# A first expert stage whose output products run as three f32r passes over split operands

## The chip, the cores and the metric

The kernel runs on one core of a Trainium2 chip. The metric is the device time of one execution in microseconds, the median of several runs. A core has TensorE (PE, with its weight loads shown as PEld), VectorE (DVE), ScalarE (ACT) and GpSimd (POOL); SyncE (SP) issues transfers. Each engine works through its own list in order, and they meet at semaphores.

## What is computed

Four pairs of attention and feed-forward layers over x of 8 x 256 tokens with 256 features. What matters here is the first feed-forward layer, a router with eight experts, one of which each token takes:

```python
logits = jnp.einsum('bsd,de->bse', x, router_W) + router_b
top1 = jnp.argmax(softmax(logits), axis=-1)
h = jax.nn.relu(jnp.einsum('bsd,edf->besf', x, W1) + b1[:, None, :])   # 256 -> 1024
y = jnp.einsum('besf,efd->besd', h, W2) + b2[:, None, :]               # 1024 -> 256
out = jnp.einsum('bse,besd->bsd', gates, y)
```

All of it is float32. The second attention, which follows, uses weights wq, wk, wv, wo that are split into a high part (rounded to the one-pass format f32r) and a low part (what rounding lost).

## The kernel before

The kernel is a row of stages, each a block in which all engines start and end together. The first expert stage is `expert_tiles` with `gated=False` and the tag `f0_`; the second expert stage is the same function with `gated=True`, and the change leaves that one alone.

`dispatch` sorts the tokens by expert into NT = 23 tiles of 128 places, each of one expert (`table` holds the expert of each tile, `order` the tokens), and loads the weights of the first two tiles (`load_first`). The weights have two slots; tile i uses slot i % 2. For each tile:

- GpSimd gathers the 128 rows of x (L1576), two tiles ahead (it waits for the turn of tile i - 2). Behind the gather it runs `beside` (L679 on): in tile order it loads the second attention's raw weights (L684), and for i from 4 to 19 it casts half a matrix to its high part (L696) or subtracts to its low part (L699), in turn. The raw weights lie in two buffers of their own, `a1_raw0` and `a1_raw1`.
- TensorE turns the rows (L1592, two transposes) into px; ScalarE copies them to xgT (L1631).
- TensorE makes the 1024 hidden values of 128 tokens in two halves of four column blocks (L1603, 16 products of float32, into ph[0] and ph[1]), then turns the rows of tile i + 1, then makes the output of tile i (L1613, eight float32 products with 256 columns, into py).
- ScalarE adds the bias and cuts at zero for half 0 (L1645, four instructions), VectorE for half 1 (L1684, four), both into hT in float32. VectorE adds b2 to the output (L1692) and ScalarE issues its store (L1653).
- SyncE loads the next weights (`load`, L1544 on): once tile i - 1 has been turned it compares the experts of tiles i and i - 2, and if they differ it issues w1 (L1549), waits until the output products of tile i - 2 are done, and issues w2 (L1555), 1 MB each. The hidden products of tile i wait for both.

So the output products of a tile come before the hidden products of the next, and a float32 product stands in the trace as two records.

Of the kernel before, what the change touches and what calls it, by code (L numbers as in the profile page):

```python
# [12 lines left out]
F32 = mybir.dt.float32  # L13
F32R = mybir.dt.float32r
# [3 lines left out]
ALU = mybir.AluOpType  # L18
ACT = mybir.ActivationFunctionType
AX = mybir.AxisListType  # L20

P = 128
B, S, D = 8, 256, 256
DK = D // P
# [4 lines left out]
E, F = 8, 1024  # L29
FT = F // P  # L30
# [635 lines left out]
                    take_out(i, 1)  # L666


def split_weights(nc, ctx, io):

    H64 = H * D1
    names = ("wq", "wk", "wv", "wo")
    shapes = ([P, DK, H64], [P, DK, H64], [P, DK, H64], [P, H64 // P, D])
    high = [ctx.enter_context(nc.sbuf_tensor("a1_%s_high" % n, s, F32R)) for n, s in zip(names, shapes)]
    low = [ctx.enter_context(nc.sbuf_tensor("a1_%s_low" % n, s, F32R)) for n, s in zip(names, shapes)]
    raw = [ctx.enter_context(nc.sbuf_tensor("a1_raw%d" % n, [P, DK * H64], F32)) for n in range(2)]
    FIRST = 4

    def beside(pool, i, loaded, made):  # L679

        def load(n):
            if n >= 2:
                pool.wait_ge(made, 4 * (n - 1))
            pool.dma_start(raw[n % 2][:, :].rearrange("p (a n) -> p a n", a=shapes[n][1]),  # L684
                           io["a1_" + names[n]].rearrange("k p n -> p k n")).then_inc(loaded, 16)

        if i in (1, 2):
            load(i - 1)
        if FIRST <= i < FIRST + 16:
            n, step = divmod(i - FIRST, 4)  # L690
            cols = slice(step // 2 * H64, (step // 2 + 1) * H64)
            h, l = (t[:, :, :].rearrange("p a n -> p (a n)")[:, cols] for t in (high[n], low[n]))
            if step == 0:
                pool.wait_ge(loaded, 16 * (n + 1))
            if step % 2 == 0:
                pool.tensor_copy(h, raw[n % 2][:, cols]).then_inc(made, 1)  # L696
            else:
                pool.wait_ge(made, 4 * n + step)
                pool.tensor_tensor(l, raw[n % 2][:, cols], h, ALU.subtract).then_inc(made, 1)  # L699
            if step == 3 and n < 2:  # L700
                load(n + 2)
    return high, low, beside
# [990 lines left out]
            every_tile(dve, finish)  # L1693


def combine(nc, top, tag, x, ys, dest, weights):

    with top.stage() as ctx:
        K = len(weights)
        yt = ctx.enter_context(nc.sbuf_tensor(tag + "yt", [P, TT, K, D], F32))  # L1700
        gathered = [top.for_indirect(tag + f"gathered{n}") for n in range(8)]
        added = top.semaphore(tag + "added")
        block = ctx.enter_context(nc.Block())

        @block.gpsimd
        def _(pool):
            for t in range(TT):
                if t >= 8:
                    pool.wait_ge(added, K * (t - 7))
                for c in range(K):  # L1710
                    pool.indirect_dma_start(yt[:, t, c, :], None, ys,
                                            bass.IndirectOffsetOnAxis(ap=dest[:, c, t:t + 1], axis=0)
                                            ).then_inc(gathered[t % 8], 16)

        @block.vector
        def _(dve):
            for t in range(TT):
                dve.wait_ge(gathered[t % 8], 16 * K * (t // 8 + 1))
                for c in range(K):
                    if c:  # L1720
                        dve.wait_ge(added, K * t + c)
                    dve.scalar_tensor_tensor(out=x[:, t, :], in0=yt[:, t, c, :], scalar=weights[c][:, t:t + 1],
                                             in1=x[:, t, :], op0=ALU.mult, op1=ALU.add).then_inc(added, 1)
# [855 lines left out]
def build(nc, io, out):  # L2579

    with ExitStack() as top:
        def sb(name, shape, dt=F32):
            return top.enter_context(nc.sbuf_tensor(name, shape, dt))

        x, xt = sb("x", [P, TT, D]), sb("xt", [P, DK, B * S])
# [4 lines left out]
        NT0, NT1 = TT + E - 1, 2 * TT + E - 1  # L2590
        table = sb("table", [1, NT1 + 2], I32)
        xs0, xs1 = (nc.dram_tensor(n, (B * S, D), F32).ap() for n in ("normed_x0", "normed_x1"))
# [35 lines left out]
        attention0(nc, stages, x, xt, io, consts, (rw0, logits, xs0), load_consts, make_consts)  # L2628
        gates0(nc, stages, logits, hot1, share1, consts)
        with ExitStack() as kept:  # L2630
            high, low, beside = split_weights(nc, kept, io)
            with ExitStack() as held:
                weights, load_first = expert_weights(nc, held, "f0_", io, gated=False)
                dispatch(nc, stages, "d0_", [hot1], dest[:, 0:1, :], table[:, 0:NT0 + 2], NT0, order[:, 0:NT0],
                         consts, load_first)
                expert_tiles(nc, stages, "f0_", xs0, ys0, table, order, NT0, io, consts, weights, gated=False,
                             beside=beside)
            attention1(nc, stages, x, xt, io, consts, (high, low), ys0, dest, share1, (rw1, logits, xs1))
        gates1(nc, stages, logits, hot1, hot2, largest1, largest2, consts)
        tail, load_ahead = load_tail(nc, top, io)  # L2640
# [78 lines left out]
```

## Time and profile before

| what | value |
|---|---|
| median of three runs | 1735.83 us (1734.33 to 1741.48) |
| the profiled execution | 1732.06 us, its span 1730.2 us |
| TensorE busy | 1479.9 us, 86% of the span |
| VectorE, ScalarE, GpSimd busy | 48%, 30%, 24% |
| first expert stage, first product to last output | 325.98 to about 500.8 us |
| granted TensorE clock, whole span | 0.93 of full speed |

The first expert stage takes a tenth of the span. The page cuts the span into 40 slices of 43 us; the ninth to the eleventh lie wholly in this stage, and TensorE shows nine tenths or more in each, VectorE two and ScalarE one or two. A busy TensorE is not TensorE at its peak: what its work costs is read from the starts of its instructions in the timeline.

### The profile page before, as it was taken

The numbers are of one execution on the slowest core, as the hardware profiler recorded it, in microseconds if no ns is written. First come the engines' busy times: TensorE is split into PE (matmuls) and PEld (weight loads), VectorE is DVE, ScalarE is ACT, GpSimd is POOL, SyncE is SP. The second block draws the span as 40 slices with busy tenths as digits, with TensorE's granted clock in tenths as the row PEclk, the third lists the DMA queues.
The fourth block names the chain that finished last, engine by engine and source line by source line (L and its number), as shares of the span: only waits on it lengthen the run. The fifth ranks groups of instructions, "written<-read, shape, count | busy, mean of one in ns | idle before, by whom it ended". The sixth has DMA issues, their size and how long they took to land. (4 is left out here: it accounts for less than half of the span.)

```text
span 1730.2 us, 31832 instructions
## 1 busy us (share of the span) xinstructions
PE 1479.9 (86%) x11282; PEld 1285.6 (74%) x11282; DVE 832.5 (48%) x2319; ACT 522.7 (30%) x1300; POOL 417.6 (24%) x651
## 2 busy tenths in 40 slices
PE   4789986599958999999994599999999978985775
PEld 3466664489957888888884599999999967864664
DVE  4677663322215666666665311111111127876996
ACT  1233332112214445445441111111111112334553
POOL 2011101133223444433322100000000036730222
PEclk7799999699989999999997699999999989996888
DMA  7655420783410000000000444224426232100000
GB/s 149 109 92 107 76 38 20 271 272 107 132 40 20 7 13 14 20 19 14 7 8 13 162 170 170 97 97 170 170 95 244 85 98 68 50 6 1 13 13 25
DMA packets 99469, 141.90 MB, mean 82 GB/s; under 512 B 10209, under 2 KB 83425, under 8 KB 99233
## 3 DMA queue, kind: packets, MB, share of 16 engines
q1 hardware_dynamic: 81968, 111.92, 22.3%
q0 software_dynamic: 6368, 18.62, 3.7%
q10 hardware_dynamic: 11024, 9.97, 1.9%
q8 instruction: 62, 1.02, 0.3%
q14 instruction: 47, 0.38, 0.1%
HBM read 113.22 MB, written 14.42 MB: 74 GB/s over the span
## 5 line engine op out<-in xcount | busy, mean ns | idle before, releaser
L1603 PEld LDWEIGHTS f_ph<-f_xgT,f_w 128*128 128x128 f32 x3232 | 374.0, 194 | 10.5 <-issue 4.2
L1603 PE MATMUL f_ph<-f_xgT,f_w 128*128 128x128 f32 x3232 | 375.3, 277 | 5.3 <-DMA f_w<-in_f_w 2.7
L1613 PE MATMUL f_py<-f_w,f_hT 128*128 128x256 f32 x992 | 224.7, 379 | 0.2 <-ACT f_hT L1645 0.2
L1613 PEld LDWEIGHTS f_py<-f_w,f_hT 128*128 128x128 f32 x992 | 183.6, 190 | 23.3 <-issue 0.8
L1677 DVE TENSOR_TENSOR f_hT<-f_ph,f_gate_o 128x512 f32<-128x512 f32 x78 | 53.9, 691 | 262.9 <-ACT f_gate_o L1639 262.9
L1576 POOL DMA_INDIRECT f_xg<-normed_x,order x62 | 59.5, 960 | 498.8 <-PE f_px L1592 464.2
L987 ACT ACTIVATE a_work<-a_ps,a_bias 128x128 f32<-128x128 f32 (+1 forms) x256 | 104.1, 419 | 172.5 <-issue 98.0
L1187 POOL TENSOR_TENSOR a_work<-a_work,a_recip 128x256 f32<-128x256 f32 (+1 forms) x128 | 103.2, 828 | 147.8 <-DVE a_recip L1106 146.7
L1639 ACT ACTIVATE f_gate_o<-f_ph 128x512 f32<-128x512 f32 x78 | 46.6, 597 | 295.2 <-PE f_ph L1603 295.1
L574 DVE CUSTOM_DVE_ANT_0 a_shut_s<-a_ps,a_neg 128x256 f32<-128x256 f32 x256 | 93.0, 419 | 39.5 <-PE a_ps L253 39.0
L486 ACT ACTIVATE a_pT<-a_ps 128x1024 f32<-128x1024 f32 x64 | 65.5, 1024 | 118.8 <-PE a_ps L253 118.8
L1111 DVE TENSOR_TENSOR a_qk<-a_ps,a_qk 128x512 fp32r<-128x512 f32 x64 | 44.2, 691 | 96.6 <-ACT a_qk L1004 96.6
L1684 DVE TENSOR_SCALAR f_hT<-f_ph,f_b 128x128 f32<-128x128 f32 x92 | 25.9, 344 | 89.5 <-PE f_ph L1603 89.5
L1088 DVE TENSOR_REDUCE a_top_s<-a_ps 128x2 f32<-128x256 f32 (+1 forms) x128 | 64.1, 542 | 6.2 <-PE a_ps L873 6.2
L2496 POOL TENSOR_TENSOR f_sq<-f_s,f_magic 128x1024 bf16<-128x1024 f32 x16 | 30.3, 1893 | 138.9 <-DVE f_s L2392 138.9
L1645 ACT ACTIVATE f_hT<-f_ph,f_b 128x128 f32<-128x128 f32 x92 | 26.2, 368 | 123.0 <-PE f_ph L1603 123.0
L873 PE MATMUL a_ps<-a_qk 64*128 64x256 f32 x768 | 62.6, 295 | 0.0
L806 PE MATMUL a_ps<-a_src,a_wq_high 128*128 128x256 f32 x256 | 58.4, 310 | 4.5 <-POOL a_src L1178 4.3
L1690 DVE COPY f_yg<-f_py 128x256 f32<-128x256 f32 x39 | 16.5, 424 | 93.4 <-PE f_py L1613 93.4
L847 PE MATMUL a_ps<-ident,a_work 128*128 128x128 f32 x384 | 53.2, 275 | 7.8 <-POOL a_work L1187 3.6
L820 PE MATMUL a_ps<-a_work,a_V 128*64 128x128 f32 x768 | 56.0, 281 | 1.8 <-issue 1.6
L431 POOL TENSOR_SCALAR a_ve<-a_mv 128x2 f32<-128x2 f32 x16 | 3.1, 191 | 225.5 <-DVE a_mv L529 202.5
(319 smaller groups left out, 2881.0 us busy)
## 6 DMA issues: line engine op xcount, KB each, us to landing
f_w<-in_f_w SPq DMA_DIRECT2D x70, 1024.0 KB, 7.8
sorted_y<-f_yg ACTq DMA_DIRECT2D x62, 128.0 KB, 1.7
a_qs<-a_part SPq DMA_DIRECT2D x48, 128.0 KB, 4.4
a_ks<-a_part SPq DMA_DIRECT2D x42, 128.0 KB, 6.2
normed_x<-a_xn SPq DMA_DIRECT2D x16, 256.0 KB, 2.1
x<-in_x SPq DMA_DIRECT2D x8, 256.0 KB, 6.6
a_mask<-in_mask SPq DMA_DIRECT2D x8, 256.0 KB, 6.4
a_maskT<-in_maskT SPq DMA_DIRECT2D x8, 256.0 KB, 6.5
```

What stands on the lines that cost most here:

```text
L486: act.activation(pT[:, u // 2 % 2, 2 * (u % 2):2 * (u % 2) + 2, :, :].rearrange("p j t n -> p j (t n)"), ps[:, ST:ST + 2, :], ACT.Exp, sca ...
L574: a = dve.tensor_tensor_reduce(out=shut_s[:, j, t, :], in0=ps[:, bank(m) + j, t * S:(t + 1) * S], in1=neg[:, m // U % 3, t, :], scale=1.0, ...
L806: mm = pe.matmul(out, left[a][c], right[b][c], start=start and i == 0, stop=stop and i == len(todo) - 1)
L820: mm = pe.matmul(o_ps[i * W:(i + 1) * W, block, :], V[:, c, h + i, :], pT[:, s, i, (c + block) * P:(c + block + 1) * P], start=(c == 0), s ...
L873: mm = pe.matmul(ps[:, SB + 2 * s + i, t * S:(t + 1) * S], qk[r, s, a, 0, t * P:(t + 1) * P], qk[r, s, b, 1, :], start=False, stop=(n == l ...
L987: act.activation(prob[:, s, i, t * P:(P if t == 0 else TRI)], ps[:, SB + 2 * s + i, t * S:(t * S + P * (t + 1))], ACT.Exp, bias=bias[:, s, ...
L1088: dve.tensor_reduce(top_s[:, s, t, :], ps[:, SB + 2 * s:SB + 2 * s + 2, t * S:t * S + P * (t + 1)], AX.X, ALU.max).then_inc(max_done, 1)
L1187: pool.tensor_tensor(part, part, recip[:, s, t, :].unsqueeze(2).to_broadcast([P, 2, P * (t + 1)]), ALU.mult).then_inc(shares_done, 1)
L1576: pool.indirect_dma_start(xg[:, i % 2, :], None, xs, bass.IndirectOffsetOnAxis(ap=order[:, i:i + 1], axis=0)).then_inc(x_ready[i % 2], 16)
L1603: mm = pe.matmul(ph[:, q, n, f * P:(f + 1) * P], w[:, s, k, (q * FQ + f) * P:(q * FQ + f + 1) * P], xgT[:, s, k, :], start=(k == 0), stop= ...
L1613: mm = pe.matmul(py[:, s, 0:D], hT[:, s, f, :], w2[:, s, f, :], start=(f == 0), stop=(f == FT - 1))
L1677: dve.tensor_tensor(hT[:, s, q * FQ:(q + 1) * FQ, :].rearrange("p f n -> p (f n)"), ph[:, q, 1, :], gate_o[:, q, :], ALU.mult).then_inc(h_ ...
```

## The change

A function of its own, `biased_tiles`, replaces `expert_tiles` in the first expert stage. Its hidden products are as before. Its output products take f32r operands: hidden tile and w2 are each split into a high part and a low part, and three products (high x high, high x low, low x high) stand for one, 24 for a tile. The parts are made as follows:

- ScalarE and VectorE evacuate ph into `raw` as before (four instructions each). ScalarE rounds both halves to the high part (`hidden_high`, 128x512), VectorE subtracts to the low part (`hidden_low`, 128x512).
- w2 of every tile is split, whether its expert is new or not: ScalarE rounds it (`weights_high`, 128x2048) behind the evacuation, the rounding and the turned rows; VectorE subtracts (`weights_low`, 128x2048) as its first work of the next tile.
- The output products of tile i - 1 run behind the hidden products of tile i and the turn of tile i + 1; for the last tile they follow at the end.
- SyncE issues w1 once the hidden products of tile i - 2 are done, and w2 once w2 of tile i - 2 has been split.
- GpSimd is as before, but the raw weights of the second attention go to `xt`, a buffer of [128, 2, 2048] float32 that is free in this stage, in place of the two raw buffers.

```diff
@@ -666,14 +666,14 @@
                     take_out(i, 1)
 
 
-def split_weights(nc, ctx, io):
+def split_weights(nc, ctx, io, spare):
 
     H64 = H * D1
     names = ("wq", "wk", "wv", "wo")
     shapes = ([P, DK, H64], [P, DK, H64], [P, DK, H64], [P, H64 // P, D])
     high = [ctx.enter_context(nc.sbuf_tensor("a1_%s_high" % n, s, F32R)) for n, s in zip(names, shapes)]
     low = [ctx.enter_context(nc.sbuf_tensor("a1_%s_low" % n, s, F32R)) for n, s in zip(names, shapes)]
-    raw = [ctx.enter_context(nc.sbuf_tensor("a1_raw%d" % n, [P, DK * H64], F32)) for n in range(2)]
+    raw = [spare[:, n, :] for n in range(2)]
     FIRST = 4
 
     def beside(pool, i, loaded, made):
@@ -681,7 +681,7 @@
         def load(n):
             if n >= 2:
                 pool.wait_ge(made, 4 * (n - 1))
-            pool.dma_start(raw[n % 2][:, :].rearrange("p (a n) -> p a n", a=shapes[n][1]),
+            pool.dma_start(raw[n % 2].rearrange("p (a n) -> p a n", a=shapes[n][1]),
                            io["a1_" + names[n]].rearrange("k p n -> p k n")).then_inc(loaded, 16)
 
         if i in (1, 2):
@@ -1691,6 +1691,222 @@
                 else:
                     dve.tensor_tensor(yg[:, s, :], py[:, s, 0:D], b2[:, e, :], ALU.add).then_inc(y_out, 1)
             every_tile(dve, finish)
+
+def biased_tiles(nc, top, tag, xs, ys, table, order, NT, io, consts, weights, beside):
+    Q = 2
+    FQ = FT // Q
+    PASSES = ((0, 0), (0, 1), (1, 0))
+    with top.stage() as ctx:
+        def sb(name, shape, dt=F32):
+            return ctx.enter_context(nc.sbuf_tensor(tag + name, shape, dt))
+
+        w1, w2, b1, b2 = (weights[n] for n in ("w1", "w2", "b1", "b2"))
+        xg, yg = sb("xg", [P, 2, D]), sb("yg", [P, 2, D])
+        xgT = sb("xgT", [P, 2, DK, P])
+        raw = sb("raw", [P, Q, FQ * P])
+        hT = [sb("h_" + n, [P, 2, FT, P], F32R) for n in ("high", "low")]
+        w2_parts = [sb("w2_" + n, [P, 2, FT, D], F32R) for n in ("high", "low")]
+        ph = ctx.enter_context(nc.psum_tensor(tag + "ph", [P, Q, 512], F32))
+        px = ctx.enter_context(nc.psum_tensor(tag + "px", [P, 512], F32))
+        py = ctx.enter_context(nc.psum_tensor(tag + "py", [P, 2, 512], F32))
...
+        def tiles(engine, body):
+
+            body(0, 0, 0, first=True)
+            with engine.Fori(0, (NT - 3) // 4) as four:
+                for j in range(1, 5):
+                    body(four * 4 + j, j % 2, four * 2 + j // 2)
+            body(NT - 2, 1, (NT - 3) // 2)
+            body(NT - 1, 0, (NT - 1) // 2, last=True)
+
+        @block.sync
+        def _(sp):
+            def load(i, s, half):
+                sp.wait_ge(h_ready, i * 2 - 2)
+                e = sp.value_load(table[0:1, bass.ds(i + 2, 1)], min_val=0, max_val=E - 1)
+                before = sp.value_load(table[0:1, bass.ds(i, 1)])
+                with sp.If(e != before):
+                    sp.dma_start(w1[:, s, :, :], io[tag + "w1"][bass.ds(e, 1)].rearrange("e (k p) f -> p (e k) f", p=P)
+                                 ).then_inc(w_ready[s], 16)
+                    sp.wait_ge(w2_low, i - 1)
+                    sp.dma_start(w2[:, s, :, :], io[tag + "w2"][bass.ds(e, 1)].rearrange("e (k p) d -> p (e k) d", p=P)
+                                 ).then_inc(w_ready[s], 16)
+                with sp.Else():
+                    sp.sem_inc(w_ready[s], 16 * NW)
+
...
+        @block.gpsimd
+        def _(pool):
+            for i in range(NT):
+                if i >= 2:
+                    pool.wait_ge(turned, i + 1)
+                pool.indirect_dma_start(xg[:, i % 2, :], None, xs,
+                                        bass.IndirectOffsetOnAxis(ap=order[:, i:i + 1], axis=0)
+                                        ).then_inc(x_ready[i % 2], 16)
+                beside(pool, i, beside_in, beside_made)
+
+        @block.tensor
+        def _(pe):
+            pe.sem_inc(turned, 2)
+            pe.sem_inc(y_ready, 2)
+
+            def turn(i, s, half):
+
+                pe.wait_ge(x_ready[s], half * 16 + 16)
+                pe.wait_ge(turned_out, i + 1)
+                for k in range(DK):
+                    mm = pe.transpose(px[:, k * P:(k + 1) * P], xg[:, s, k * P:(k + 1) * P], consts["ident"][:, :])
+                mm.then_inc(turned, 1)
+
+            def hidden(i, s, half):
+                pe.wait_ge(turned_out, i + 2)
+                pe.wait_ge(w_ready[s], (half + 1) * (16 * NW))
+                for q in range(Q):
+                    pe.wait_ge(h_out[q], i + 1)
+                    for f in range(FQ):
+                        for k in range(DK):
+                            mm = pe.matmul(ph[:, q, f * P:(f + 1) * P], w1[:, s, k, (q * FQ + f) * P:(q * FQ + f + 1) * P],
+                                           xgT[:, s, k, :], start=(k == 0), stop=(k == DK - 1))
+                    mm.then_inc(h_ready, 1)
+
+            def output(i, s):
+                pe.wait_ge(h_low, i * 2 + 2)
+                pe.wait_ge(w2_low, i + 1)
+                pe.wait_ge(y_out, i + 1)
+                for f in range(FT):
+                    for n, (a, b) in enumerate(PASSES):
+                        mm = pe.matmul(py[:, s, 0:D], hT[a][:, s, f, :], w2_parts[b][:, s, f, :],
+                                       start=(f == 0 and n == 0), stop=(f == FT - 1 and n == len(PASSES) - 1))
+                mm.then_inc(y_ready, 1)
+
+            def multiply(i, s, half, first=False, last=False):
+                hidden(i, s, half)
+                if not last:
+                    turn(i + 1, 1 - s, half + s)
+                if not first:
+                    output(i - 1, 1 - s)
+                if last:
+                    output(i, s)
+
+            turn(0, 0, 0)
+            tiles(pe, multiply)
+
+        @block.scalar
+        def _(act):
...
+            def turn_out(i, s):
+                act.wait_ge(turned, i + 3)
+                act.activation(xgT[:, s, :, :].rearrange("p k n -> p (k n)"), px[:, 0:D], ACT.Copy
+                               ).then_inc(turned_out, 1)
+
+            def weights_high(i, s, half):
+                act.wait_ge(w_ready[s], (half + 1) * (16 * NW))
+                act.wait_ge(y_ready, i + 1)
+                act.activation(w2_parts[0][:, s, :, :], w2[:, s, :, :], ACT.Copy).then_inc(w2_high, 1)
+
+            def hidden_high(i, s, q):
+                act.wait_ge(h_out[q], i + 2)
+                act.activation(hT[0][:, s, q * FQ:(q + 1) * FQ, :].rearrange("p f n -> p (f n)"), raw[:, q, :], ACT.Copy
+                               ).then_inc(h_high, 1)
+
+            def store(i, s):
+                act.wait_ge(y_out, i + 3)
+                act.dma_start(ys[bass.ds(i * P, P), :], yg[:, s, :]).then_inc(stored[s], 16)
+
+            def gate(i, s, half, first=False, last=False):
+                e = act.value_load(table[0:1, bass.ds(i + 2, 1)], min_val=0, max_val=E - 1)
+                act.wait_ge(h_ready, i * 2 + 1)
+                if not first:
+                    act.wait_ge(h_low, i * 2 - 1)
+                for f in range(FQ):
+                    a = act.activation(raw[:, 0, f * P:(f + 1) * P], ph[:, 0, f * P:(f + 1) * P], ACT.Relu,
+                                       bias=b1[:, e, f:f + 1])
+                a.then_inc(h_out[0], 1)
+                hidden_high(i, s, 0)
+                if not last:
+                    turn_out(i + 1, 1 - s)
+                hidden_high(i, s, 1)
+                weights_high(i, s, half)
+                if not first:
+                    store(i - 1, 1 - s)
+                if last:
+                    store(i, s)
+
...
+        @block.vector
+        def _(dve):
...
+            def weights_low(i, s):
+                dve.wait_ge(w2_high, i + 1)
+                dve.tensor_tensor(w2_parts[1][:, s, :, :], w2[:, s, :, :], w2_parts[0][:, s, :, :], ALU.subtract
+                                  ).then_inc(w2_low, 1)
+
+            def hidden_low(i, s, q):
+                dve.wait_ge(h_high, i * 2 + (q + 1))
+                dve.tensor_tensor(hT[1][:, s, q * FQ:(q + 1) * FQ, :].rearrange("p f n -> p (f n)"), raw[:, q, :],
+                                  hT[0][:, s, q * FQ:(q + 1) * FQ, :].rearrange("p f n -> p (f n)"), ALU.subtract
+                                  ).then_inc(h_low, 1)
+
+            def take_out(i, s, half):
+                e = dve.value_load(table[0:1, bass.ds(i + 2, 1)], min_val=0, max_val=E - 1)
+                dve.wait_ge(y_ready, i + 3)
+                dve.wait_ge(stored[s], half * 16 + 16)
+                dve.tensor_tensor(yg[:, s, :], py[:, s, 0:D], b2[:, e, :], ALU.add).then_inc(y_out, 1)
+
+            def finish(i, s, half, first=False, last=False):
+                if not first:
+                    weights_low(i - 1, 1 - s)
+                e = dve.value_load(table[0:1, bass.ds(i + 2, 1)], min_val=0, max_val=E - 1)
+                dve.wait_ge(h_ready, i * 2 + 2)
+                if not first:
+                    dve.wait_ge(h_low, i * 2)
+                for f in range(FQ):
+                    a = dve.tensor_scalar(raw[:, 1, f * P:(f + 1) * P], ph[:, 1, f * P:(f + 1) * P],
+                                          b1[:, e, FQ + f:FQ + f + 1], 0.0, ALU.add, ALU.max)
+                a.then_inc(h_out[1], 1)
+                hidden_low(i, s, 0)
+                hidden_low(i, s, 1)
+                if not first:
+                    take_out(i - 1, 1 - s, half + (s - 1))
+                if last:
+                    weights_low(i, s)
+                    take_out(i, s, half)
+
+            tiles(dve, finish)
...
@@ -2628,13 +2844,12 @@
         attention0(nc, stages, x, xt, io, consts, (rw0, logits, xs0), load_consts, make_consts)
         gates0(nc, stages, logits, hot1, share1, consts)
         with ExitStack() as kept:
-            high, low, beside = split_weights(nc, kept, io)
+            high, low, beside = split_weights(nc, kept, io, xt)
             with ExitStack() as held:
                 weights, load_first = expert_weights(nc, held, "f0_", io, gated=False)
                 dispatch(nc, stages, "d0_", [hot1], dest[:, 0:1, :], table[:, 0:NT0 + 2], NT0, order[:, 0:NT0],
                          consts, load_first)
-                expert_tiles(nc, stages, "f0_", xs0, ys0, table, order, NT0, io, consts, weights, gated=False,
-                             beside=beside)
+                biased_tiles(nc, stages, "f0_", xs0, ys0, table, order, NT0, io, consts, weights, beside)
             attention1(nc, stages, x, xt, io, consts, (high, low), ys0, dest, share1, (rw1, logits, xs1))
         gates1(nc, stages, logits, hot1, hot2, largest1, largest2, consts)
         tail, load_ahead = load_tail(nc, top, io)
```

## Rows read from the trace of the kernel before

**Rows 1.** The page, costliest groups: busy us, mean ns | idle before, its releaser.

```profile
L1613 PE MATMUL f_py<-f_w,f_hT 128*128 128x256 f32 x992 | 224.7, 379 | 0.2 <-ACT f_hT L1645 0.2
```

**Rows 2.** Timeline of TensorE: start, duration, merged instructions, [idle before <- releaser].

```profile
325.98 5.48 PE L1603 MATMUL f_ph<-f_xgT,f_w 128*128 128x128 f32 x32 [0.66 <-ACT f_xgT L1631]
...
375.07 3.84 PE L1603 MATMUL f_ph<-f_xgT,f_w 128*128 128x128 f32 x32 [2.07 <-DMA f_w<-in_f_w]
...
493.10 3.73 PE L1603 MATMUL f_ph<-f_xgT,f_w 128*128 128x128 f32 x32
```

**Rows 3.** Timeline of VectorE, the stage's last output.

```profile
500.43 0.42 DVE L1692 TENSOR_TENSOR f_yg<-f_py,f_b 128x256 f32<-128x256 f32 x1 [2.31 <-PE f_py L1613]
```

**Rows 4.** Timeline of tile 11, and of a GpSimd subtraction two tiles later.

```profile
411.58 3.73 PE L1603 MATMUL f_ph<-f_xgT,f_w 128*128 128x128 f32 x32
...
415.15 0.38 PE L1592 MATMUL f_px<-ident,f_xg 128*128 128x128 f32 x2
...
415.37 3.62 PE L1613 MATMUL f_py<-f_w,f_hT 128*128 128x256 f32 x16
415.49 1.13 DVE L1684 TENSOR_SCALAR f_hT<-f_ph,f_b 128x128 f32<-128x128 f32 x4 [3.07 <-PE f_ph L1603]
...
415.81 0.97 POOL L1576 DMA_INDIRECT f_xg<-normed_x,order  x1 [3.91 <-PE f_px L1592]
416.78 1.05 POOL L696 CAST a_wv_high<-a_raw 128x1024 fp32r<-128x1024 f32 x1
...
418.83 3.73 PE L1603 MATMUL f_ph<-f_xgT,f_w 128*128 128x128 f32 x32
419.14 0.42 DVE L1692 TENSOR_TENSOR f_yg<-f_py,f_b 128x256 f32<-128x256 f32 x1 [2.52 <-PE f_py L1613]
...
424.02 2.36 POOL L699 TENSOR_TENSOR a_wv_low<-a_raw,a_wv_high 128x1024 fp32r<-128x1024 f32 x1
```

**Rows 5.** One stretch: its length, busy us by engine, then PEclk, DMA share, GB/s.

```profile
334.00:505.00 171.00, 162.11 (x1104) 150.51 (x1102) 34.53 (x111) 33.10 (x109) 47.52 (x38) 1.00 0.48 157
```

**Rows 6.** Timeline of SyncE's queue: first and last of nine w1 issues.

```profile
333.22 0.18 SPq L1549 DMA_DIRECT2D f_w<-in_f_w  x1
...
453.54 0.13 SPq L1549 DMA_DIRECT2D f_w<-in_f_w  x1
```

**Rows 7.** The line L1555 (w2's loads, both expert stages).

```profile
DMA to landing us min/median/max: 6.9/7.8/8.1
```

**Rows 8.** Timeline of GpSimd, its third raw load.

```profile
365.77 0.75 POOL L684 DMA_DIRECT2D a_raw<-in_a_wv  x1 [0.30 <-POOL a_wq_low L699]
```

**Rows 9.** Timeline of TensorE in the second attention, first and last of six.

```profile
616.16 0.28 PE L806 MATMUL a_ps<-a_wo_high,a_o_high 128*128 128x256 f32 x1
...
616.75 0.28 PE L806 MATMUL a_ps<-a_wo_low,a_o_high 128*128 128x256 f32 x1
```

**Rows 10.** Groups of ScalarE by shape.

```profile
L955 ACT ACTIVATE a_src<-a_ctx_raw 128x512 fp32r<-128x512 f32 x8 | 5.0, 630 | 0.0
...
L2221 ACT ACTIVATE t_w1q<-t_w 128x2048 fp32r<-128x2048 f32 x1 | 1.9, 1919 | 0.0
```

**Rows 11.** Groups of VectorE by shape.

```profile
L1958 DVE TENSOR_REDUCE m_asum<-t_w 128x1 f32<-128x2048 f32 x2 | 4.5, 2272 | 0.0
...
L1980 DVE TENSOR_TENSOR m_cbs<-t_cb,m_scale 128x512 f32<-128x512 f32 x1 | 0.7, 693 | 0.0
```

**Rows 12.** Timeline of the second dispatch, GpSimd and VectorE.

```profile
950.26 3.42 POOL L1404 TENSOR_TENSOR d_numbers<-d_in_tile,token 128x1248 bf16<-128x1248 bf16 x1 [16.84 <-DVE d_in_tile L1399]
951.47 4.57 DVE L1462 TENSOR_TENSOR d_at_slot<-index,d_slot 128x512 bf16<-128x512 f32 x4
```

**Rows 13.** The line L1462: durations in ns, min/median/max.

```profile
L1462 DVE TENSOR_TENSOR d_at_slot<-index,d_slot x12: 672/679/2762, 313.6 to 959.0; 128x512 bf16<-128x512 f32 x12
```

**Rows 14.** The line L1549 (w1's loads, both expert stages).

```profile
DMA to landing us min/median/max: 4.9/5.3/6.7
```

**Rows 15.** Timeline of TensorE in the first attention.

```profile
40.99 1.11 PE L358 MATMUL a_ps<-ident,a_xn 128*128 128x128 f32 x4 [3.83 <-DVE a_xn L537]
```

More of the change, by code:

```diff
@@ L1693, in _ @@
             every_tile(dve, finish)
+def biased_tiles(nc, top, tag, xs, ys, table, order, NT, io, consts, weights, beside):
+    NW = 2
+    Q = 2
[13 more added lines that the diff above has]
+        py = ctx.enter_context(nc.psum_tensor(tag + "py", [P, 2, 512], F32))
+        x_ready = [top.for_indirect(tag + "x_ready%d" % n) for n in range(2)]
+        (w_ready0, w_ready1, turned, turned_out, h_ready, h_out0, h_out1, h_high, h_low, w2_high, w2_low,
+         y_ready, y_out, stored0, stored1) = (top.semaphore(tag + n) for n in (
+             "w_ready0", "w_ready1", "turned", "turned_out", "h_ready", "h_out0", "h_out1", "h_high", "h_low", "w2_high", "w2_low",
+             "y_ready", "y_out", "stored0", "stored1"))
+        beside_made = top.semaphore(tag + "beside_made")
+        beside_in = top.for_indirect(tag + "beside_in")
+        w_ready, h_out, stored = (w_ready0, w_ready1), (h_out0, h_out1), (stored0, stored1)
+        block = ctx.enter_context(nc.Block())
+        def tiles(engine, body):
[19 more added lines that the diff above has]
+                    sp.sem_inc(w_ready[s], 16 * NW)
+            for s in range(2):
+                sp.wait_ge(weights["first"][s], weights["arrivals"][s])
+                sp.sem_inc(w_ready[s], 16 * NW)
+            with sp.Fori(1, NT // 2) as pair:
+                load(pair * 2, 0, pair)
+                load(pair * 2 + 1, 1, pair)
+            if NT % 2:
+                load(NT - 1, 0, NT // 2)
+        @block.gpsimd
[48 more added lines that the diff above has]
+        def _(act):
+            act.sem_inc(turned_out, 1)
+            act.sem_inc(h_out[0], 1)
+            act.wait_ge(weights["first"][0], weights["arrivals"][0])
+            def turn_out(i, s):
[31 more added lines that the diff above has]
+                    store(i, s)
+            act.sem_inc(stored[0], 16)
+            act.sem_inc(stored[1], 16)
+            turn_out(0, 0)
+            tiles(act, gate)
+            act.wait_ge(stored[0], 16 + 16 * ((NT + 1) // 2))
+            act.wait_ge(stored[1], 16 + 16 * (NT // 2))
+        @block.vector
+        def _(dve):
+            dve.sem_inc(y_out, 2)
+            dve.sem_inc(h_out[1], 1)
+            dve.wait_ge(weights["first"][0], weights["arrivals"][0])
+            def weights_low(i, s):
[31 more added lines that the diff above has]
+            tiles(dve, finish)
```

## The prediction

> **What bounds the kernel now.** I read the page first. The output products of the two expert stages (L1613) are one of TensorE's largest groups, 225 us in 992 records [rows 1]. The change touches only the first expert stage, so the timeline of that stage came next: 23 tiles, the first product at 325.98 us, the last output taken at 500.43 us [rows 2, 3]. A tile whose weights are there already shows what sets its length [rows 4]: hidden products from 411.58, the turn of the next tile at 415.15, output products at 415.37, next hidden products at 418.83. That is 7.25 us without a gap on TensorE: 3.57 + 0.22 + 3.46. ScalarE, VectorE and GpSimd wait for TensorE in between. The granted clock is 1.00 from 334 to 505 us, the 2.4 GHz level [rows 5]. Then the loads: nine tiles change expert and fetch 2 MB each, w1 and w2, in three runs: tiles 2, 3, 4, then 6 to 9, then 17, 18; the rows show the first and the last of the nine w1 issues [rows 6]. There a w2 row lands 6.9 to 8.1 us after its issue [rows 7], about one tile, and TensorE waits now and then, most at tile 6 (2.07 us), where GpSimd's own load of 1 MB (L684) had been issued at the same moment as w2 [rows 2, 8]. Between the rest of the tiles TensorE has next to no gap. So the stage is bound by TensorE, with the weight loads close behind.
>
> **The gain: fewer passes.** An f32 product of 256 columns stands as two records; 16 records take 3.46 us, 0.216 each [rows 4]. The new output is 24 products with f32r operands. Their like are in the second attention: six with fresh weights each start from 616.16 to 616.75, five steps, 0.118 each [rows 9]. 24 x 0.118 = 2.83 us. A tile saves 0.63 us, its length becomes 6.62 us, and 23 tiles save 14.5 us. This is the whole gain, and the bound of it: the turn and the hidden products stay as they are.
>
> **The new work beside it.** I count from the start of tile j's hidden products as zero. VectorE's four evacuations start at 3.9 as now and end at 5.05 [rows 4]. ScalarE rounds the second half of the hidden tile (128x512 from SBUF, 0.63) to 5.75, then all of w2 (128x2048, 1.92) to 7.7 [rows 10]. VectorE subtracts one half of the hidden tile at 5.1, the other at 5.8 (0.69 each, to 6.5), takes out the output of tile j-1 (0.42) at 6.9, and subtracts w2 from 7.75. The 128x2048 reduction took 2.27 and the 128x512 subtraction of the like operands 0.69 [rows 11]; I take 2.3, so the low part of w2 is there at 10.05. TensorE asks for it at 6.62 + 3.8 = 10.4. So it is hidden, with 0.35 us to spare. The loop through both engines (evacuate 1.13, round 0.63, round w2 1.92, subtract 2.3, some 0.3 of waits and the expert's number) is 6.3 us, under 6.62. All four steps are at nothing, under the cover of TensorE; without the cover each costs its full length.
>
> **What GpSimd does to it.** GpSimd gathers the rows (415.81, 0.97) and then casts (1.04) or subtracts (2.36) for the next attention, eight of each, subtractions in tiles 2, 4, ... 16 [rows 4]. Before, nothing of VectorE with two SBUF operands ran there; now three such instructions do. In the second dispatch GpSimd's product at 950.26 ran for 3.42 us, to 953.68. Of the four VectorE instructions with two SBUF operands that start at 951.47 one took 2.76 us, where the median is 0.68 [rows 12, 13]: it ends 0.5 us behind GpSimd's, as if it had started when that ended. So one waits for the other's end. Here GpSimd is ready at 5.2, waits for the first subtraction to 5.8, and holds until 6.85 (cast) or 8.2 (subtraction). With a cast w2's low part is late by 0.2 (10.25), still hidden. With a subtraction: second half 8.2 to 8.9, take-out to 9.3, w2 to 11.6. TensorE waits 1.2 us, and no later work gives it back.
> The Trainium skill (SBUF — State Buffer, "Who interferes with whom") says that a VectorE instruction with two SBUF inputs and a GpSimd instruction that reads SBUF exclude each other for a whole instruction. By that rule these f32 and f32r forms are blocked as the bf16 one of the row was; were it an oddity of that row, the sum would be 11 us lower (third rival).
>
> **What the loads do.** SyncE's load of w2 for tile i now waits for w2's subtraction of tile i-2, not for its output products. It issues at 10.1 us behind the start of tile i-2 (11.7 where GpSimd subtracts) instead of at 7.3. TensorE's hidden products ask for both loads at 13.2. SyncE is in order, so w1 of tile i+1 also stands behind this wait; its own condition (hidden products of tile i-1 done) comes at about 11.7, so it rarely loses. By then w1 of tile i, issued at 5.1, is in. So w2 travels as w1 does now, with the next load issued 1 to 2 us behind: 4.9 to 6.7 us, median 5.3 [rows 14]. The upper bound is 8.1 [rows 7]. I take 5.3, and 6.7 for tile 6, beside GpSimd's load. The stall is then 10.1 + 5.3 - 13.2 = 2.2 us, or 3.8 behind a GpSimd subtraction. It is not paid twice in a row: after a late tile the next has that time in hand. It falls on tiles 2, 4, 6, 8, and 17 or 18, and GpSimd's subtractions stand before four of these.
>
> **The two ends.** At the start output products move behind the next hidden ones, so tile 1 starts at 332.3 (hidden products of tile 0 run 5.48 from 325.98 [rows 2], then turn and its copy). At the end the last tile has no cover: hidden products to 3.6, output of the tile before to 6.4, then TensorE is idle until w2's low part at 10.1. At full clock the last output is taken at 13.3 behind its tile's start; now at 7.33 (493.10 to 500.43 [rows 2, 3]). After an idle time of 3.83 us four transposes took 1.11 us [rows 15], where the turn of two takes 0.38 at the full clock [rows 4]; so I charge the last 24 products at the 1.2 GHz level, 2.8 us more, between nothing and 2.8.
>
> **The sum,** as starts of tiles. w2(2) is issued when tile 0 is split, at 337.9: T2 = 343.2. T3 = +6.6 = 349.8. T4 = T2 + 11.7 + 5.3 = 360.1. T5 = 366.7. T6 = T4 + 11.7 + 6.7 = 378.5. T7 = 385.1. T8 = T6 + 17.0 = 395.5. T9 = 402.1. From T9 to T16 seven tiles: 7 x 6.62 + 4 x 1.2 (GpSimd subtractions in tiles 8, 10, 12, 14) = 51.1: T16 = 453.2. T18 = T16 + 17.0 = 470.2. T22 = +26.5 = 496.6. Last output 496.6 + 13.3 + 2.8 = 512.7, against 500.43: 12.3 us later. Behind it the store and the next stage follow as now. The other parts (xt in place of the raw buffers, which no one else uses here) I cost at nothing; GpSimd's gathers are issued two tiles ahead of their use. The profiled execution took 1732.06 us with its span of 1730.2; the median of the three runs is 1735.83. The difference is added to the median: 1748.1 us.
>
> **Rivals.**
> 1. Faster, the saving comes through: w2's load is in before TensorE asks. The point that decides is a landing of 13.2 - 10.1 = 3.1 us; and VectorE has time for GpSimd. Then -14.5 and, for the end without cover, +3.2: 11.3 us less, 1724.5. Against it: no row lands under 4.9. Chance 0.07.
> 2. w2 travels as slowly as w2 rows do now, 8.1 us: 2.8 more on four stalls and 1.4 on tile 6, 12.6 in all: 1760.7. For it: these are w2's own rows, in 1 KB pieces; against it: they had an own w1 ahead. Chance 0.13.
> 3. VectorE and GpSimd don't block each other in these forms. T4 = 358.6, T6 = 375.4, T8 = 390.8, T16 = 443.7, T18 = 459.1, T22 = 485.6, end 501.7 with the slow clock: 1.3 us later, 1737. Chance 0.20.
> 4. The loop of ScalarE and VectorE becomes the bound: with 0.6 us of waits in place of 0.3 a tile is 6.9, and 13 tiles outside the loads' stalls lose 0.3 each, 4 us: 1752. Chance 0.10.
> 5. The forecast: 0.50.
>
> **Range and chances.** 8.7 us (0.5%) is about what a measurement of this kernel can tell from no change. Faster needs rival 1 or nearly: 0.08. Same holds rival 3 and the low end of the forecast (clock kept at the end, GpSimd late enough to hurt less): 0.32. Slower: 0.60. The range reaches from below rival 3 to rival 2: 1733 to 1761.
>
> **What would show it.** Right: output products with starts 0.118 apart; w2's load issued about 10 us behind the start of the tile two before; TensorE waiting for DMA by 2 to 4 us at tiles 2, 4, 6, 8; the 128x512 or 128x2048 subtractions on VectorE showing maxima near 3 us or more, or GpSimd's growing, in even tiles; 3 to 4 us of idle TensorE before the last output. Wrong: GpSimd's and VectorE's SBUF work side by side at unchanged lengths; a landing of w2 under 4.9 us; tiles above 7 us where GpSimd only casts.

## The result and the profile after

| | median | profiled execution | first expert stage |
|---|---|---|---|
| before | 1735.83 us | 1732.06 us | 174.9 us |
| after | 1754.29 us (1750.55 to 1756.34) | 1755.35 us | 196.3 us |

The change is slower: the ratio to the kernel before is 1.0105, with a 95% interval of 1.0082 to 1.0128, 18.5 us between the medians. The last column is read from the two timelines, from the first hidden product of tile 0 to the end of the last take-out, in which VectorE adds b2 to the last output: 325.98 to 500.85 before [rows 2, 3], 328.03 to 524.32 after. The stage is 21.4 us longer. Of the 23.3 us between the two profiled executions 2.05 lie ahead of the stage, in code that is the same; behind it nothing changes.

The groups of the page, costliest first, with busy us, mean ns, and idle before with its releaser, that answer to [rows 1]:

```profile
L1790 PE MATMUL f_ph<-f_xgT,f_w 128*128 128x128 f32 x736 | 97.4, 297 | 16.7 <-DMA f_w<-in_f_w 15.5
...
L1800 PE MATMUL f_py<-f_w_high,f_h_high 128*128 128x256 f32 x184 | 54.7, 297 | 10.0 <-issue 6.5
```

Both wait now: the hidden products (L1790) 15.5 us for transfers, the output products (L1800) 10.0 us, of which 3.3 stand before the last tile's output, where nothing covers the split. The mean of a hidden product has grown to 297 ns. Where, the timeline of TensorE shows. These are the hidden products of tiles 2, 3, 4 and 6, and the first output product of tile 12 (answers to [rows 2]; start, duration, merged instructions, idle before):

```profile
346.11 5.37 PE L1790 MATMUL f_ph<-f_xgT,f_w 128*128 128x128 f32 x32 [2.96 <-DMA f_w<-in_f_w]
...
354.41 3.74 PE L1790 MATMUL f_ph<-f_xgT,f_w 128*128 128x128 f32 x32
...
365.28 5.47 PE L1790 MATMUL f_ph<-f_xgT,f_w 128*128 128x128 f32 x32 [3.00 <-DMA f_w<-in_f_w]
...
384.56 6.56 PE L1790 MATMUL f_ph<-f_xgT,f_w 128*128 128x128 f32 x32 [3.05 <-DMA f_w<-in_f_w]
...
447.87 0.39 PE L1800 MATMUL f_py<-f_w_high,f_h_high 128*128 128x256 f32 x1 [0.75 <-DVE f_w_low L1875]
```

Tiles 2, 4, 6 and 8 wait about 3.0 us for a load, and the same 32 records that take 3.74 us elsewhere take 5.4 to 6.6 behind the wait. In every second tile, up to tile 14, the output products stand 0.7 to 0.8 us idle until w2's low part is there. (The trace puts some of these down to "issue"; at tile 10, for one, VectorE's subtraction of w2 ends at 433.46 and the output products start at 433.56.) The stretches of the trace name the reason. The columns are as in [rows 5]; the third number from the end is the granted clock:

```profile
346.00:350.00 4.00, 3.89 (x21) 3.89 (x22) 0.03 (x1) 0.09 (x1) 0.00 (x0) 0.58 1.01 362
...
384.00:390.00 6.00, 5.44 (x25) 5.44 (x26) 1.02 (x1) 1.41 (x5) 0.00 (x0) 0.50 0.97 337
...
405.00:411.00 6.00, 6.00 (x29) 6.00 (x30) 0.00 (x0) 1.77 (x5) 0.00 (x0) 0.52 0.87 314
411.00:516.00 105.00, 98.21 (x841) 96.71 (x840) 86.90 (x119) 64.62 (x114) 29.92 (x22) 1.00 0.26 82
```

Before, the clock was 1.00 from 334 us to the end of the stage [rows 5]. Now it is at the 1.2 GHz level (0.50) for a time behind each of the four waits: 0.58 is the mean of a stretch in which it came back. Behind the fourth of them it is 1.00 again up to 516 us. w2's load, in SyncE's queue for tile 4 and by its line (answers to [rows 6, 7]):

```profile
352.80 0.38 SPq L1743 DMA_DIRECT2D f_w<-in_f_w  x1
359.09 0.37 SPq L1746 DMA_DIRECT2D f_w<-in_f_w  x1
```

```profile
DMA to landing us min/median/max: 5.4/6.1/7.4
```

w1 leaves 6.7 us behind the start of tile 2, w2 13.0 behind it. And VectorE with GpSimd, in tile 10 and over the stage (answer to [rows 12, 13]):

```profile
427.09 3.83 DVE L1880 TENSOR_TENSOR f_h_low<-f_raw,f_h_high 128x512 fp32r<-128x512 f32 x2
...
427.35 2.41 POOL L699 TENSOR_TENSOR a_wv_low<-xt,a_wv_high 128x1024 fp32r<-128x1024 f32 x1
```

```profile
L1880 DVE TENSOR_TENSOR f_h_low<-f_raw,f_h_high x46: 677/692/3236, 335.1 to 515.0; 128x512 fp32r<-128x512 f32 x46
```

Two subtractions, 0.69 us each at the median, take 3.83 together, with GpSimd's 2.41 in between.

### The profile page after: what moved, and what is told of

Its sections match the earlier page's. It is cut to its first block and busy times, and to the rows that moved or that the text cites. A ratio compares the mean times of both kernels' runs of the same rounds, so it can differ in the third digit from the quotient of the medians.

```text
span 1753.5 us, 32455 instructions
## 1 busy us (share of the span) xinstructions
PE 1482.2 (85%) x11466; PEld 1295.4 (74%) x11466; DVE 939.6 (54%) x2388; ACT 591.0 (34%) x1369; POOL 420.5 (24%) x651
## 5 line engine op out<-in xcount | busy, mean ns | idle before, releaser
L1603 PEld LDWEIGHTS f_ph<-f_xgT,f_w 128*128 128x128 f32 x2496 | 286.9, 193 | 3.0 <-issue 1.1
L1603 PE MATMUL f_ph<-f_xgT,f_w 128*128 128x128 f32 x2496 | 287.2, 276 | 0.7 <-ACT f_xgT L1631 0.7
L1613 PE MATMUL f_py<-f_w,f_hT 128*128 128x256 f32 x624 | 141.1, 379 | 0.0
L1613 PEld LDWEIGHTS f_py<-f_w,f_hT 128*128 128x128 f32 x624 | 115.5, 190 | 14.1
L1790 PE MATMUL f_ph<-f_xgT,f_w 128*128 128x128 f32 x736 | 97.4, 297 | 16.7 <-DMA f_w<-in_f_w 15.5
L1790 PEld LDWEIGHTS f_ph<-f_xgT,f_w 128*128 128x128 f32 x736 | 94.8, 212 | 18.5 <-DMA f_w<-in_f_w 14.8
L1800 PE MATMUL f_py<-f_w_high,f_h_high 128*128 128x256 f32 x184 | 54.7, 297 | 10.0 <-issue 6.5
```

The lines of the kernel that those rows point to most:

```text
L1603: mm = pe.matmul(ph[:, q, n, f * P:(f + 1) * P], w[:, s, k, (q * FQ + f) * P:(q * FQ + f + 1) * P], xgT[:, s, k, :], start=(k == 0), stop= ...
L1613: mm = pe.matmul(py[:, s, 0:D], hT[:, s, f, :], w2[:, s, f, :], start=(f == 0), stop=(f == FT - 1))
L1790: mm = pe.matmul(ph[:, q, f * P:(f + 1) * P], w1[:, s, k, (q * FQ + f) * P:(q * FQ + f + 1) * P], xgT[:, s, k, :], start=(k == 0), stop=(k ...
L1800: mm = pe.matmul(py[:, s, 0:D], hT[a][:, s, f, :], w2_parts[b][:, s, f, :], start=(f == 0 and n == 0), stop=(f == FT - 1 and n == len(PASS ...
```

## The experiments

The length of the stage is read as above, from one execution of each kernel. Two executions of one and the same kernel (`split_first_store_late` and `store_late_again`, below) gave 165.8 and 169.4 us, so a difference of a few us between two stages counts only where the rows show what it is made of. Kernels are built on the change unless named otherwise.

**Is the late load of w2 enough by itself? `before_late_w2`.** The kernel before, one wait changed.

```diff
-                    sp.wait_ge(y_ready, i + 1)
+                    sp.wait_ge(h_ready, i * 2) if not gated else sp.wait_ge(y_ready, i + 1)
```

> The kernel before with one wait changed: w2 of tile i is issued when the hidden products of tile i-1 are done, 3.6 us before TensorE asks for it, in place of 7.2. No split, no f32r, nothing else. Theory (a late w2 load alone makes most of the loss): w2 lands in about 6 us, each of the nine loading tiles waits about 2.4 us, against 6 us for all of them before: about 15 us more, 1751 us, and up to 10 more if the clock falls in these waits. Rival (the loss is in the split itself and its blocking): within 3 us of before, 1736 to 1739.

Measured: ratio 1.0125 (1.0080 to 1.0169), 1754.3 against 1733.6 us; stage 198.6 us, 23.8 more than before. This one wait costs as much as the whole change: TensorE stands idle 1.7 to 2.8 us ahead of each of the nine loading tiles, 19.1 us together, against 4.0 before. Tile 6, whose w2 was issued at 373.49:

```profile
373.51 3.62 PE L1613 MATMUL f_py<-f_w,f_hT 128*128 128x256 f32 x16
379.97 6.71 PE L1603 MATMUL f_ph<-f_xgT,f_w 128*128 128x128 f32 x32 [2.84 <-DMA f_w<-in_f_w]
```

The loads of w2 land in 5.5 to 6.4 us, the wait is there, and the hidden products take 6.71 us in place of 3.73: the granted clock is 0.50 from 380 to 386 us. Tiles 7, 9 and 18 are slow as well (5.4 to 5.5 us). No split is in this kernel, so a late load is enough by itself for a loss of this size. It doesn't say that the split and its blocking cost nothing in the change; that is read from the next runs.

**Is it the clock that stretches the hidden products? `fill_the_wait`.**

```diff
+            def fill(i, s):
+                e = pe.value_load(table[0:1, bass.ds(i + 3, 1)], min_val=0, max_val=E - 1)
+                before = pe.value_load(table[0:1, bass.ds(i + 1, 1)])
+                with pe.If(e != before):
+                    for n in range(10):
+                        pe.matmul(spare[:, 0:D], consts["identb"][:, :], consts["tri"][:, :, :],
+                                  start=True, stop=True)
...
+                if not first and not last:
+                    fill(i, s)
```

> The change with ten spare products of 256 columns (their result is not used) on TensorE behind the output products, only where the next tile loads weights. Theory (the clock falls because TensorE is idle for 3 us): idle time before tiles 2, 4, 6, 8 falls from 3.0 to about 1.8 us, their hidden products take 3.7 us in place of 5.4 to 6.6, the loads land as before: some 9 us less, 1745 us. Rival (these long hidden products come from something else, for instance transfers that write beside them): they stay at 5.4 to 6.6 us and the time at 1754.

Measured: 1744.3 us, ratio 1.0070 (1.0047 to 1.0092); stage 186.6 us, 9.7 less than the change. Tile 6 again:

```profile
372.76 1.27 PE L1810 MATMUL f_spare<-tri,identb 128*128 128x256 bf16 x10
376.09 3.84 PE L1791 MATMUL f_ph<-f_xgT,f_w 128*128 128x128 f32 x32 [2.06 <-DMA f_w<-in_f_w]
```

The transfer still ends the wait, but 1.27 us of spare work stands in it, 2.06 us are idle, and the hidden products take 3.84. The same holds for tiles 2, 4 and 8: 3.84 us each, with 1.2 to 1.6 us of idle time. Transfers beside the products are as before (369 GB/s beside those of tile 2, at a granted clock of 1.00, against 362 GB/s with the change, at 0.58), so they are not what stretched them. The 9.7 us are what is left on balance: the four tiles give back 8.7 us of slow products and their loads are issued earlier, while the spare products ahead of tiles 3, 7 and 9, which had nothing to wait for, cost 1.2 us each.

**Does the blocking of VectorE and GpSimd cost time? `gpsimd_behind`.**

```diff
+                if i >= 4:
+                    pool.wait_ge(w2_low, i - 2)
                 beside(pool, i, beside_in, beside_made)
```

> The change with GpSimd's cast or subtraction held until VectorE has split w2 of the tile before, so that they don't meet VectorE's two subtractions of the hidden tile. Theory (the two block each other): no subtraction of VectorE over 1.5 us, no wait of TensorE for w2's low part in tiles 9 to 16 (4 x 1.0 us), w2's loads for tiles 4, 6, 8 issued 1.3 us earlier, which may also keep the clock: 4 to 13 us less, about 1744. Rival (the blocking costs nothing that sets the end): 1752 or more.

Measured: 1744.6 us, ratio 1.0053 (1.0022 to 1.0083); stage 189.5 us, 6.8 less. The subtractions' line:

```profile
L1882 DVE TENSOR_TENSOR f_h_low<-f_raw,f_h_high x46: 678/686/1261, 339.1 to 512.2; 128x512 fp32r<-128x512 f32 x46
```

No subtraction takes more than 1.26 us, and tiles 10 to 16 start 6.66 us apart without exception. In the change every second one of them is 7.7. So the blocking sets the length of these tiles. But GpSimd's third raw load now left later, 5.9 us behind the start of tile 5, and tile 7 had 4.04 us of idle time ahead of it, where the change has none: part of the gain went there. That the raw load did it was not tried by itself here; raw_load_later, below, has the like.

**Are the two separate? `fill_and_behind`.** Both edits.

> The change with both the spare products in the waits (fill_the_wait) and GpSimd's work held behind w2's subtraction (gpsimd_behind). If the clock and the blocking are separate losses, the gains add up but for the tiles where the earlier load had already kept the clock: from 1754 some 9 less and some 8 less, 1737 us. If they are the same loss, no better than either alone, 1744 us. What is left over the kernel before (about 3 us) would be the late loads and the end without cover, less the saved passes.

Measured: 1738.7 us, ratio 1.0040 (1.0022 to 1.0058); stage 181.4 us, 15.0 less than the change, where the two alone gave 9.7 and 6.8. In the stages they add up but for 1.5 us. The ratios are less clear: by them the two alone give back 6 and 9 us and both together 11, and the interval overlaps that of `gpsimd_behind` alone. What shows two losses are the rows: in this trace no hidden products behind tile 0 take more than 3.84 us, and tiles 10 to 16 start 6.66 to 6.69 us apart.

**What is left without loads? `no_reload` and `before_no_reload`.** SyncE only counts up the semaphore, in the change and in the kernel before. All tiles then use the weights of the first two, so the output is another one and only this stage can be compared, in one execution of each.

```diff
-                with sp.If(e != before):
...
+                sp.sem_inc(w_ready[s], 16 * NW)
```

> The change without any weight load after the first two tiles (all tiles of the first expert stage use those experts' weights, so the output is another; the routing of the second expert stage changes with it, so only the first stage is to be read). Theory: tiles of 6.66 us, 1.04 more in the eight with a GpSimd subtraction, all hidden products 3.7 us; from the first product to the last output 6.7 + 148.2 + 14.7 = 169.6 us. Rival (the tiles themselves have become longer than before, loads or not): over 175.

> The kernel before without any weight load after the first two tiles (same remark on its output). Tiles of 7.25 us, from the first product to the last output 9.0 + 152.2 + 7.8 = 169.0 us: without loads the change and the kernel before are equal, the saved passes having been paid for the blocking (8 x 1.04) and the end without cover. Rival: the change is faster by 8 us or more here, if blocking and end cost less than I think.

Measured: stage 170.0 us with the change and 170.1 us before. The last tile's hidden products on TensorE and the last take-out on VectorE, first of the change, then of the kernel before:

```profile
488.80 3.74 PE L1783 MATMUL f_ph<-f_xgT,f_w 128*128 128x128 f32 x32
...
501.97 0.42 DVE L1881 TENSOR_TENSOR f_yg<-f_py,f_b 128x256 f32<-128x256 f32 x1 [3.35 <-PE f_py L1793]
```

```profile
486.32 3.73 PE L1606 MATMUL f_ph<-f_xgT,f_w 128*128 128x128 f32 x32
...
493.66 0.42 DVE L1695 TENSOR_TENSOR f_yg<-f_py,f_b 128x256 f32<-128x256 f32 x1 [2.31 <-PE f_py L1616]
```

Without loads the saved passes pay for the blocking and the end without cover to within 0.1 us. Loads add 4.8 us to the stage before (174.9) and 26.3 us to that of the change (196.3). So the loss against the kernel before appears only with the loads, and 9.7 of it is what the spare products give back. The blocking is in the stage with and without them (eight tiles of 7.6 to 7.7 us in `no_reload`) and takes 8 us of the 13 that the shorter tiles save.

**Is the order the cause, then? `split_first`.** ScalarE rounds w2 of tile i, and VectorE subtracts, ahead of the tile's own evacuations.

```diff
             def gate(i, s, half, first=False, last=False):
                 e = act.value_load(table[0:1, bass.ds(i + 2, 1)], min_val=0, max_val=E - 1)
+                weights_high(i, s, half)
...
-                weights_high(i, s, half)
...
-                if not first:
-                    weights_low(i - 1, 1 - s)
+                weights_low(i, s)
```

> The change with w2's split moved ahead of the tile's own evacuations: ScalarE rounds w2 of tile i before it evacuates tile i, VectorE subtracts before it evacuates. Theory (late w2 loads, and the TensorE clock that falls in the stall, are what the change lost): w2 of tile i is split at about 4.4 us behind the tile's start in place of 12 to 14, SyncE issues the load of w2 two tiles on some 8 us earlier, the 3.0 us waits at tiles 2, 4, 6, 8 shrink to what they were before the change (2 us and less), all hidden products take 3.7 us, and the shorter tiles come through: 1725 to 1730 us. Rival A (transfers bound the runs of loads whatever the order: 2 MB a tile in shorter tiles): waits of about 3 us stay, 1745 us or more. Rival B (VectorE and GpSimd blocking each other is the main loss): it stays as it is, about 1745.

Measured: 1774.4 us, ratio 1.0228 (1.0201 to 1.0256); stage 217.9 us. None of the three expectations held: I had put a rounding behind a wait without asking what that wait hangs on. The rows of ScalarE:

```profile
430.80 0.34 ACTq L1839 DMA_DIRECT2D sorted_y<-f_yg  x1
431.85 1.91 ACT L1830 ACTIVATE f_w_high<-f_w 128x2048 fp32r<-128x2048 f32 x1 [2.50 <-issue]
433.67 1.12 ACT L1848 ACTIVATE f_raw<-f_ph,f_b 128x128 f32<-128x128 f32 x4
434.83 0.63 ACT L1834 ACTIVATE f_h_high<-f_raw 128x512 fp32r<-128x512 f32 x1
435.36 0.36 ACT L1824 ACTIVATE f_xgT<-f_px 128x256 f32<-128x256 f32 x1
```

The store of tile i-1 waits until VectorE has taken that output out, and the rounding, the evacuation and the turned rows of the next tile stand behind this store. VectorE takes it out last of all, behind w2's subtraction, which waits for the rounding, and behind the evacuation. Its rows of tile 20, where GpSimd has no more work beside it:

```profile
518.52 2.29 DVE L1875 TENSOR_TENSOR f_w_low<-f_w,f_w_high 128x2048 fp32r<-128x2048 f32 x1 [3.25 <-ACT f_w_high L1830]
520.73 1.12 DVE L1897 TENSOR_SCALAR f_raw<-f_ph,f_b 128x128 f32<-128x128 f32 x4
521.77 1.47 DVE L1880 TENSOR_TENSOR f_h_low<-f_raw,f_h_high 128x512 fp32r<-128x512 f32 x2
523.37 0.42 DVE L1888 TENSOR_TENSOR f_yg<-f_py,f_b 128x256 f32<-128x256 f32 x1
```

The rounding began at 516.58, the store follows at 523.96 and the next rounding at 525.09, 8.5 us behind the first. The output itself was done on TensorE at 519.0. So the ring runs through ScalarE and VectorE, and not through TensorE's products as the expectation of the next run has it. TensorE waits for the turned rows in most tiles from tile 6 on; tiles are 8.4 us and more from tile 4 on. Beside GpSimd it is worse: w2's subtraction for tile 10, at 422.65, takes 5.00 us, the evacuation stands behind it, and TensorE is idle for 2.05 us inside the hidden products of tile 11.

**`split_first_store_late`.** The same, and the store that ScalarE issues in tile i is that of tile i-2.

```diff
-                if not first:
-                    store(i - 1, 1 - s)
+                if not first and not second:
+                    store(i - 2, s)
```

> As split_first, and ScalarE issues the store of tile i-2 in tile i, where that output has long been taken out, in place of that of tile i-1, whose wait stood ahead of the rounding of the next w2. In split_first this wait closed a ring: rounding of w2 of tile i, turned rows of tile i+1, hidden products, output products, take-out, store, rounding of w2 of tile i+1, some 8.5 us where TensorE alone needs 6.7. Theory (late w2 loads and the clock are what the change lost): ring gone, tiles without a load 6.7 us, w2's loads issued within 5 us of the start of the tile two before, waits at tiles 2, 4, 6, 8 at 2 us or less, clock kept; stage of 164 to 168 us against 174.9 before: 1723 to 1729 us. Rival A (transfers bound the loading tiles whatever the order, and more so with shorter tiles): waits of 3 us, over 1740.

Measured: 1724.0 us, ratio 0.9950 (0.9931 to 0.9969): faster than both kernels. The stage takes 165.8 us, 9.1 less than before and 30.5 less than with the change. SyncE's queue for tile 6, and its hidden products:

```profile
359.09 0.39 SPq L1743 DMA_DIRECT2D f_w<-in_f_w  x1
359.67 0.37 SPq L1746 DMA_DIRECT2D f_w<-in_f_w  x1
```

```profile
370.68 3.84 PE L1790 MATMUL f_ph<-f_xgT,f_w 128*128 128x128 f32 x32 [3.16 <-DMA f_w<-in_f_w]
```

w2 leaves 0.6 us behind w1 and lands in 7.5 to 11.0 us, slower than with the change (5.4 to 7.4), but it has the time. Tiles 2, 4 and 17 wait 1.7, 0.8 and 0.6 us, tile 6 3.2, tile 8 only 0.1. A subtraction of VectorE still takes up to 3.1 us beside GpSimd, but it has room: tiles 10 to 16 are 6.66 us apart. Rival A falls: 2 MB a tile do come through, save at tile 6. Of the 30.5 us against the change some 9 are waits for transfers, 9 slow products, 7 the blocking, and the rest lies at the two ends (the last take-out ends 11.6 us behind the last tile's start, not 15.1): the order lessens every one of the losses, not the late load alone.

**What is tile 6 waiting for? `raw_load_later`, beside `store_late_again`** (split_first_store_late once more, on the same chip).

```diff
-            if step == 3 and n < 2:
-                load(n + 2)
+            if i == 10:
+                load(2)
+            if i == 13:
+                load(3)
```

> split_first_store_late, and GpSimd loads the second attention's third and fourth raw weights (1 MB each) behind the gathers of tiles 10 and 13 in place of 7 and 11, clear of the runs of expert loads. Theory: the 3.2 us wait at tile 6 was this transfer beside w1 and w2 (the only loading tile with a third transfer, and w2 took up to 11 us to land); it falls to about 1 us, the time by some 2 us, 1722 us. Rival: the wait at tile 6 stays, and the time is the same within the noise.

> split_first_store_late once more, beside raw_load_later on the same chip, so that 2 us can be told: 1724 us.

Measured: 1732.2 us (1.0001, 0.9981 to 1.0021) and 1728.3 us (0.9962, 0.9947 to 0.9977), with stages of 169.1 and 169.4 us. The expected gain of 2 us is not there: the median is 3.9 us higher. The wait at tile 6 fell from 3.2 to 0.5 us, as the theory says, but one of 3.6 us stands at tile 9, after GpSimd's load at 380.56: GpSimd runs ahead, and "tile 10" on its list is tile 7 on TensorE's, still among the loads. So a wait of some 3 us went with the raw load in both places; a place clear of the expert loads was not tried. The second run repeats the gain over the kernel before, 0.4% in place of 0.5, with a stage 5.5 us shorter than before in place of 9.1.

## Why the prediction was nearly right, and what it left out

Point by point, from the start of the stage:

- **The gain.** Right. Starts of f32r products are 0.12 apart, tiles without load or blocking 6.66 us (6.62 forecast).
- **The new work in cover.** Right without loads: rounding 1.90, subtraction 2.28, and where GpSimd only casts, TensorE doesn't wait for w2.
- **GpSimd.** Right: 1.04 us in each tile with a subtraction (1.2 forecast), T16 - T9 = 50.7 us (51.1 forecast). What the row with the one blocked instruction showed holds for f32 and f32r forms too: 3.83 us for two subtractions around GpSimd's 2.41. The Trainium skill's rule that the forecast named (SBUF — State Buffer, "Who interferes with whom") agrees with this trace.
- **The loads.** Right in place: waits at tiles 2, 4, 6 and 8, none at 3, 5, 7, 9; of 17 and 18 one was forecast, and both wait (1.8 us each). Landing was sized at 5.3 us and measured 6.1 at the median. T4 - T2 was 19.2 us where 17.0 was forecast; 1.6 of the difference are the slow products of tile 2.
- **The clock in these waits.** This is the term that failed. I priced a fallen clock only for the last output products and took the four waits of 2 to 4 us at full clock, though the row for it stood among mine [rows 15]. The hidden products behind them took 5.37, 5.47, 6.56 and 6.62 us, 9.1 more than 4 x 3.74. And the slow products delay the next split: w2 for tiles 6 and 8 left 13.1 and 14.2 us behind the tile two before, not 11.7; with the spare products it is 11.4 for tiles 4, 6 and 8.
- **The end.** Last take-out 14.7 us behind the last tile's start, 16.1 forecast. The last 24 products took 4.6 us against 3.1 for those just before them, so the slower clock cost 1.5 us and not 2.8.

Forecast for the stage: +12.3. The clock adds 9.1. The rest comes to nothing, by luck: the start and the loads are some 1.8 us later than forecast, the end 1.4 and the blocking 0.4 us earlier. That makes 21.4. The time of 1754.3 lay 6 us above the forecast and inside the range, on the slower side as said. Rival 1 (w2 there before TensorE asks) is excluded by the four waits, rival 2 (landings of 8.1 us) is excluded by w2's line, 7.4 at most, rival 3 (no blocking) and rival 4 (a bound in ScalarE and VectorE) by gpsimd_behind and by the 6.66 us tiles.

The settled cause: the new w2 load is issued behind the split, at the end of the chain, and comes too late. It costs 3 us of waiting in four tiles and 1.8 in two, 15.5 us in all against some 4 before, and 9.1 us of slow products behind these waits. The order, not the three passes, is at fault: with w2 split first and the store out of its way the same passes are 0.4 to 0.5% faster than the kernel before, in two sets of runs. That order also takes away the blocking and shortens the uncovered end, so its whole gain is not the price of the late load.

## What to carry to other kernels

When work is moved behind "everything the next tile needs", list what waits for that work to free a buffer: here a 1 MB load for two tiles on, whose issue moved from 7 to 13 us behind the tile's start. Price a wait on TensorE of 2 to 3 us with the slow products that may follow it, which can double it, and remember that they delay the next load in turn. And ask of each wait that a step is put behind what it hangs on: one store's wait turned a stage 9 us shorter into one 43 us longer.

## What was not expected of the hardware

The clock behind a wait is not settled by its length. In split_first_store_late tile 6 waited 3.16 us and its hidden products took 3.84 us. In store_late_again, the same program, the row is:

```profile
373.39 6.53 PE L1790 MATMUL f_ph<-f_xgT,f_w 128*128 128x128 f32 x32 [3.17 <-DMA f_w<-in_f_w]
```

That is 2.7 us in one place, out of the 3.6 by which the two stages differ. Waits of 2.0 us went both ways too: in gpsimd_behind one of 2.01 was followed by products of 5.46 us, one of 1.97 by 3.84. And ahead of the last tile's output the idle time is 3.3 us both with the change and in `no_reload`, but the 24 products behind it take 4.6 us in the one and 3.1 in the other. What decides was not found out.
